# A decoder layer on one core: the roots of two layer norms on GpSimd instead of ScalarE, and the activation tables fetched elsewhere

## The reference, cut to what matters

```python
def _layernorm(x, axis=-1, eps=1e-05):
    m = jnp.mean(x, axis=axis, keepdims=True)
    v = jnp.var(x, axis=axis, keepdims=True)
    return (x - m) / jnp.sqrt(v + eps)
...
x = x + _L0_attn_ref(_layernorm(x, axis=-1), ...)
x = x + _L0_xattn_ref(_layernorm(x, axis=-1), itok_BxS_13_99985, ctx_2048, ctx_2048, ctx_2048)
x = x + _L0_ffn_ref(_layernorm(x, axis=-1), ...)
```

## Time and profile before

| | |
|---|---|
| three runs, us | 590.84, 592.22, 588.93 |
| median, us | 590.84 |
| the profiled execution, us | 591.11 |
| its span, first to last instruction, us | 589.4 |
| busy in the span | PE 511.3 (87%), PEld 453.0 (77%), DVE 426.6 (72%), ACT 288.2 (49%), POOL 233.5 (40%) |
| granted TensorE clock, mean | 0.935 |

### The profile page before, as it was taken

The page is one execution under the profiler, slowest core; times in us unless marked ns, Lnnn a source line. Parts: engine busy times, 40 slices in busy tenths (PEclk is TensorE's granted clock), DMA queues, the critical chain, the costliest instruction groups (busy, mean ns, idle before and its releaser), DMA issues.

```text
span 589.4 us, 11588 instructions
## 1 busy us (share of the span) xinstructions
PE 511.3 (87%) x3291; PEld 453.0 (77%) x3292; DVE 426.6 (72%) x967; ACT 288.2 (49%) x785; POOL 233.5 (40%) x221
## 2 busy tenths in 40 slices
PE   5899999999999999999997679997837999999800
PEld 5688898998998989989887677886625888888600
DVE  5689988989889888898899776568685444444542
ACT  2466656556666666566654625444400444444400
POOL 4307413313123042131384004445005666777773
PEclk9789999999999999999999888999875999999955
DMA  7252211202102122020072009991101455423642
GB/s 214 65 138 55 63 29 51 65 1 83 32 27 62 27 53 62 14 75 0 0 237 86 2 2 296 296 264 37 36 2 35 136 156 147 134 82 112 193 135 89
DMA packets 60893, 52.91 MB, mean 90 GB/s; under 512 B 5545, under 2 KB 58623, under 8 KB 60800
## 3 DMA queue, kind: packets, MB, share of 16 engines
q1 hardware_dynamic: 55752, 43.90, 25.3%
q0 software_dynamic: 4704, 8.44, 5.8%
q10 hardware_dynamic: 408, 0.20, 0.1%
HBM read 46.21 MB, written 14.68 MB: 103 GB/s over the span
## 4 chain that ended last, share of the span: by engine, by line
PE 54%; DVE 19%; issue 9%; POOL 9%; ACT 4%; DMA 3%; POOLq 1%; DVEq 0%; ACTq 0%
PE bank L723 14%; PE bank L724 13%; PE bank L725 13%; PE bank L893 5%; POOL yg L639 5%; POOL xg_last L628 3%; DVE qk_lo L1245 3%; PE bank L801 3%; DVE rmax L1260 3%; DVE nmax L1264 3%; PE bank L901 2%; ACT qk_hi L1082 2%; DMA x_in<-in_x 2%; ACT prob L1098 1%; DVE pT_lo L1281 1%
## 5 line engine op out<-in xcount | busy, mean ns | idle before, releaser
L527 POOL TENSOR_TENSOR w_lo<-st_c,w_hi 128x512 fp32r<-128x512 f32 x32 | 41.2, 1287 | 220.7 <-ACT w_hi L1052 220.7
L1098 ACT ACTIVATE prob<-bank,nmax 128x256 f32<-128x256 f32 x128 | 59.5, 470 | 111.2 <-DVE nmax L1264 111.2
L893 PE MATMUL bank<-moe_w,xT 128*128 x256 | 67.6, 388 | 0.0
L723 PE MATMUL bank<-hT_hi,w_lo 128*128 128x512 f32 x128 | 53.9, 421 | 7.8 <-DVE qk_lo L1245 4.2
L1340 DVE TENSOR_TENSOR hid<-bank,sg 128x128 f32<-128x128 f32 x72 | 20.9, 291 | 53.4 <-ACT sg L1164 52.7
L1245 DVE SCALAR_TENSOR_TENSOR qk_lo<-bank,b_col,qk_hi 128x512 fp32r<-128x512 f32 x64 | 47.8, 747 | 13.2 <-ACT qk_hi L1082 12.2
L1260 DVE TENSOR_REDUCE rmax<-bank 128x2 f32<-128x512 f32 x64 | 43.9, 686 | 15.8 <-PE bank L725 15.2
L1164 ACT ACTIVATE sg<-bank 128x128 f32<-128x128 f32 x72 | 19.8, 277 | 70.0 <-PE bank L893 69.9
L1273 DVE TENSOR_SCALAR prob<-prob,rinv 128x256 f32<-128x256 f32 x128 | 52.0, 448 | 2.3
L724 PE MATMUL bank<-hT_lo,w_hi 128*128 128x512 f32 x128 | 51.6, 403 | 0.0
L725 PE MATMUL bank<-hT_hi,w_hi 128*128 128x512 f32 x128 | 51.4, 402 | 0.0
(11 more groups left out here) (187 smaller groups left out, 1609.0 us busy)
## 6 DMA issues: line engine op xcount, KB each, us to landing
y_dram<-ysb SPq DMA_DIRECT2D x64, 128.0 KB, 2.4
moe_w<-in_w_gate SPq DMA_DIRECT2D x8, 512.0 KB, 8.5
moe_w<-in_w_up SPq DMA_DIRECT2D x8, 512.0 KB, 7.2
moe_w<-in_w_down SPq DMA_DIRECT2D x4, 1024.0 KB, 8.8
st_c<-in_wq_codes SPq DMA_DIRECT2D x16, 128.0 KB
st_c<-in_wv_codes SPq DMA_DIRECT2D x8, 256.0 KB
st_c<-in_wo_codes SPq DMA_DIRECT2D x8, 256.0 KB
st_s<-in_wo_scales SPq DMA_DIRECT2D x16, 128.0 KB
```

Of the source, the lines that this page charges most:

```text
L723: pe.matmul(o, l_lo, r_hi, start=start, stop=False, skip_group_check=share)
L893: mm = pe.matmul(bG[n % 2][:, 0:2 * FI], xT_of(kt), w, start=kt == 0, stop=kt == KT - 1)
L1098: ex = act.activation(prob[:, i % 4, qt, :], bS[i % 2][:, qt * S:(qt + 1) * S], ACT.Exp, bias=nmax[:, i % 2, qt:qt + 1], scale=SCALE, accu ...
```

## The change

- In the second and third norm GpSimd computes `rstd` as `var` to the power of minus one half (`ln_root`, a tensor_tensor with a constant tile of -0.5 filled at the start). ScalarE's root and VectorE's reciprocal of these two norms go. The Newton step stays. The first norm is as it was.
- The two powers of the second norm stand in GpSimd's queue ahead of the mask products, the two of the third norm behind them and ahead of the index fills.
- Behind attention's last exponential ScalarE fetches the silu table, not the square root's. Behind the shared expert's silu 1 it fetches the sigmoid's.
- The sigmoid now stands ahead of the shared expert's silu 2, and VectorE's product 2 stands behind the search for the largest scores.

```diff
@@ constants @@
+        minus_half = sb("minus_half", [P, NT])
...
-        LN_STEPS = 2 * HT + 1 + 5 + HT
+        LN_STEPS = [2 * HT + 1 + 5 + HT] + 2 * [2 * HT + 1 + 4 + HT]
+
+        def ln_done(n, half):
+
+            return 2 * sum(LN_STEPS[:n]) + (half + 1) * LN_STEPS[n]
...
@@ GpSimd @@
+        def ln_root(pool, n, half):
+
+            pool.wait_ge(v_ln, ln_done(n, half) - LN_STEPS[n] + 2 * HT + 1)
+            hs = slice(half * HT, (half + 1) * HT)
+            pool.tensor_tensor(rstd[:, hs], var[:, hs], minus_half[:, hs], ALU.pow).then_inc(p_root, 1)
...
+            pool.memset(minus_half[:, :], -0.5)
...
+            ln_root(pool, 1, 0)
+            ln_root(pool, 1, 1)
             pool.wait_ge(p_mask, 2 * NROUTE - 2)
             for n in range(RSTEPS):
...
+            ln_root(pool, 2, 0)
+            ln_root(pool, 2, 1)
             pool.wait_ge(t_y, RSTEPS)
@@ VectorE, reciprocals @@
-                dve.wait_ge(a_sd, 2 * n + half + 1)
-                k = base + 2 * HT + 1
-                dve.reciprocal(rstd[:, hs], sd[:, hs]).then_inc(v_ln, 1)
+                k = base + 2 * HT + (1 if n else 2)
+                if n == 0:
+                    dve.wait_ge(a_sd, half + 1)
+                    dve.reciprocal(rstd[:, hs], sd[:, hs]).then_inc(v_ln, 1)
+                    dve.wait_ge(v_ln, k)
+                else:
+                    dve.wait_ge(p_root, 2 * (n - 1) + half + 1)
@@ ScalarE @@
                         if pl.last and i == PAIRS - 1:
-                            fetch_table(act, ACT.Sqrt)
+                            fetch_table(act, ACT.Silu)
...
-            ln_scalar(act, 1, 0)
             ln_high(act, 1, 0, ENDS[0])
-            ln_scalar(act, 1, 1)
-            fetch_table(act, ACT.Silu)
...
-            ln_scalar(act, 2, 0)
             routed_high(RSTEPS - 1)
...
-            ln_scalar(act, 2, 1)
             silu(0, 0)
             silu(1, 1)
+            fetch_table(act, ACT.Sigmoid)
             rows_copy(1, 0)
             hidden_copy(0, 0)
             hidden_copy(1, 1)
-            silu(2, 2)
             act.wait_ge(t_r, 1)
             act.activation(score[:, :, :].rearrange("p t e -> p (t e)"), bank[0][:, 0:NT * NE], ACT.Sigmoid).then_inc(a_r, 1)
+            silu(2, 2)
             silu(3, 3)
@@ VectorE, router @@
-            product(2, 2)
...
             for t in range(NT):
                 ins = dve.max(top[:, t, :], sel[:, t, :])
             own(ins)
+            product(2, 2)
             product(3, 3)
```

More of the change, by code:

```diff
@@ L339, in decoder_layer @@
         a_sd = sem("a_sd")
+        p_root = sem("p_root")
         t_ln, a_ln, v_lnlo = sem("t_ln"), sem("a_ln"), sem("v_lnlo")
@@ L489, in _ @@
                 ts = slice(half * HT, (half + 1) * HT)
-                sp.wait_ge(v_ln, (4 + half + 1) * LN_STEPS)
+                sp.wait_ge(v_ln, ln_done(2, half))
                 sp.dma_start(h_dram.rearrange("(t p) d -> p t d", p=P)[:, ts, :], h_row[:, ts, :]).then_inc(d_h, 16)
@@ L644, in ln_vector @@
         def ln_vector(dve, n, half, src):
-            base = (2 * n + half) * LN_STEPS
+            base = ln_done(n, half) - LN_STEPS[n]
             tiles = range(half * HT, (half + 1) * HT)
@@ L662, in reciprocals @@
             def reciprocals():
-                dve.wait_ge(a_sd, 2 * n + half + 1)
-                k = base + 2 * HT + 1
-                dve.reciprocal(rstd[:, hs], sd[:, hs]).then_inc(v_ln, 1)
+                k = base + 2 * HT + (1 if n else 2)
[5 more added lines that the diff above has]
+                    dve.wait_ge(p_root, 2 * (n - 1) + half + 1)
+                dve.tensor_tensor(nt1[:, hs], rstd[:, hs], rstd[:, hs], ALU.mult).then_inc(v_ln, 1)
                 dve.wait_ge(v_ln, k + 1)
-                dve.tensor_tensor(nt1[:, hs], rstd[:, hs], rstd[:, hs], ALU.mult).then_inc(v_ln, 1)
+                dve.tensor_tensor(nt1[:, hs], nt1[:, hs], var[:, hs], ALU.mult).then_inc(v_ln, 1)
                 dve.wait_ge(v_ln, k + 2)
-                dve.tensor_tensor(nt1[:, hs], nt1[:, hs], var[:, hs], ALU.mult).then_inc(v_ln, 1)
+                dve.tensor_scalar(nt1[:, hs], nt1[:, hs], -0.5, 1.5, ALU.mult, ALU.add).then_inc(v_ln, 1)
                 dve.wait_ge(v_ln, k + 3)
-                dve.tensor_scalar(nt1[:, hs], nt1[:, hs], -0.5, 1.5, ALU.mult, ALU.add).then_inc(v_ln, 1)
+                dve.tensor_tensor(rstd[:, hs], rstd[:, hs], nt1[:, hs], ALU.mult).then_inc(v_ln, 1)
                 dve.wait_ge(v_ln, k + 4)
-                dve.tensor_tensor(rstd[:, hs], rstd[:, hs], nt1[:, hs], ALU.mult).then_inc(v_ln, 1)
-                dve.wait_ge(v_ln, k + 5)
             def rows():
@@ L687, in ln_scalar @@
         def ln_scalar(act, n, half):
-            act.wait_ge(v_ln, (2 * n + half) * LN_STEPS + 2 * HT + 1)
+            act.wait_ge(v_ln, ln_done(n, half) - LN_STEPS[n] + 2 * HT + 1)
             hs = slice(half * HT, (half + 1) * HT)
@@ L700, in ln_tensor @@
                     t = half * HT + i
-                    pe.wait_ge(v_ln, (2 * n + half + 1) * LN_STEPS - HT + i + 1)
+                    pe.wait_ge(v_ln, ln_done(n, half) - HT + i + 1)
                     mm = pe.transpose(banks[kt][:, i * P:i * P + P], h_row[:, t, kt * P:kt * P + P], ident[:, :])
```

## The result

The changed kernel takes 593.62 us, the kernel before 589.03 us (medians of 18 runs each). The ratio is put at 1.0065, 95% interval 1.0045 to 1.0085, which is 2.7 to 5.0 us slower, with 3.8 in the middle; the two medians by themselves lie 4.6 us apart. The prediction said 594.1 us, +3.27, and slower as the likeliest side. The interval leaves no doubt of slower, but its lower end is under the 0.5% that the prediction took as the least that a measurement can tell.

The account below looks back on a forecast made before the run. Mostly matmul (TensorE 54% of the chain), but VectorE's third-norm steps, the logits and GpSimd's gather set the end. 0.14 - 0.05 + 2.98 + 0.2 = +3.27 on 590.84 gives 594.1 us; 8-in-10 range 587.3 to 598.0.

Parts of the forecast that it names:

- D: Third norm, half 1: variance no longer held by index fills, but `h_row` held by them instead; +2.98 us.
- X: Time of one GpSimd power on 128x4, not in the trace: taken as 0.5 us, bounds 0.188 and 1.30.
- A: Second norm, half 0: power and two hand-overs replace root and reciprocal; +0.14 us, generally X - 0.36.
- C: Third norm, half 0: root's table load goes, but the power delays VectorE's low part; -0.05 us, generally X - 0.55.
- B: Second norm, half 1: root and a table load leave the first silu's way, covered by TensorE's matmuls; nothing.
- E: Router: sigmoid table load already hidden by the logits, product 3 starts one pitch later before the index search; +0.2 us.
- the first: Rival at third norm, half 1: fills don't hold `h_row`; time 587.2 to 588.6 us; chance 0.2.
- The second: Rival on the power: slow, computed element by element, 2 to 3 us each; time 598.6 to 601.6 us; chance 0.1.
- The third: Rival at third norm, half 1: two or three rows get through between `iota_s` and `iota_tc`; 592.0 us; chance 0.15.

Follow-up runs that it names:

- e1: Changed kernel with one more wait, so GpSimd's four index fills start only after the last `h_row` of D; ratio to the kernel before 0.9944.
- e6: Kernel before with the power in the third norm alone, second norm and router as before; ratio to before 1.0033, once more 1.0032.
- e11: Changed kernel with an unused 128x32 power on constants between D's power and the index fills; ratio to the kernel before 0.9928.
- e3: Kernel before with only the change's new router order; ratio to before 0.9924, once more 0.9995.
- e4: Changed kernel with the router's order as before and no fetch of the sigmoid table; ratio to the kernel before 1.0049.

## Why the prediction was right, point by point

The sum named the right term, and its total, +3.27, is near the measured +3.8 and the stretch's +3.47. But three of its terms were mis-sized, and they cancel, which is luck: with the power's true time alone put in, the sum would have been +4.8. That 594.1 lies so near 593.62 is luck as well. It started from the 590.84 of three runs, 1.8 above the median of 18, and added a difference 1.3 smaller than that of the medians.

- **D, right in mechanism and size.** With the measured power the prediction's own terms give -2.12 + (0.12 + 1.01 - 0.49) + 4.97 = +3.49; the profile has +3.46. It put the last row 8.2 us behind the first Newton product, and it ends 8.18 behind (407.57 to 415.75). e1, e6 and e11 show that this is the fills and that it is the third norm.
- **X, the price of a power, mis-sized.** The power was taken as 0.5 us, near the 128x4 copy's 0.188, because "the start of the instruction should be most of it". It is 1.01, inside the bounds, and e11 makes plain why the copy was the wrong neighbour: by the estimate there most of it is the elements, 4 x 0.157. A is then +0.69 and not +0.14 (1.17 against 0.48 us); its formula X - 0.36 gives +0.65.
- **C, the step that failed.** "It reads SBUF as the mask product does", so a power would hold the low part until it ends. It doesn't: `pT_lo` started at 398.71 beside the power of 398.67 and took 0.70. From the start of the variance to the Newton product it is 2.39 us instead of 2.91, so C gained 0.52, where the prediction's X - 0.55 would make it lose 0.46 at the measured X.
- **B, nothing, right in the total.** The rows there were held by mask products for 2.0 us, which the prediction didn't see; its cover, TensorE's matmuls, took it up.
- **E, right alone, short in company.** The order costs 0.20 us by itself (e3), as predicted, but 0.46 in the changed kernel, where product 3 starts 0.46 behind product 2 and not 0.2, with 0.17 of it idle and released by nothing that the profile shows. All five kernels that have powers in both norms and the new order show it (2.73 or 2.74 us from score to search). Why is open. That the sigmoid's load was hidden is right; e4 shows it.
- **TensorE, left out.** In this pair of profiles about 0.6 us came back that no term named: some 0.3 between A and D (A's +0.69 and C's -0.52 should make +0.17, and the profile has -0.11) and 0.35 between the last row and the score. Neither repeats in the other profiles (55.38 to 56.86 us for the first on unchanged code, 4.78 to 5.53 for the second with D's rows held alike, by where the clock came back). Nothing shows that these 0.6 us belong to the change, and so this part of the agreement is luck too.

Together: 3 x 0.51 for X, -0.98 for C, +0.26 for E and -0.63 for TensorE make +0.18, which with 3.27 is the stretch's 3.45 to within rounding.

Of the rivals, the first (the fills leave `h_row` alone) fell by its own mark: the first `h_row` of D took 4.02 us and not 0.4. The rule of the Trainium skill (SBUF — State Buffer, SBUF: two separate sides) beside it frees a VectorE operation with two SBUF inputs from a GpSimd operation that doesn't read SBUF. The trace agrees for the Newton product at 407.77, 0.16 us beside `iota_e`; `h_row`, one tile with two scalars per partition, was held and so isn't such an operation. The second (2 to 3 us a power) fell on its figure, though its reason, computed element by element, is what e11 points to. The third fell: the second row was held by `iota_tc` until 415.12.

## What to carry to other kernels

Work that nobody waits for isn't free where it stands: before moving a wait into a queue, list what is queued behind it and ask which operation of the other engine each of these will now meet. Here one wait ahead of the fills was worth more (0.9%) than the whole rearrangement of roots and tables cost (0.65%), in both kernels. And when a disputed operation's price is bounded by a neighbour, choose one that does the same arithmetic, or measure it at two sizes.

## What the runs showed of the hardware that was not expected

- A GpSimd power on 128x4 takes 1.01 us (1.05 at A) and on 128x32 5.41 us, and it holds neither a tensor_tensor of VectorE with two SBUF inputs (0.70 us beside it, as alone) nor a tensor_scalar (four rows in 1.38 us).
- GpSimd's multiplication of 128x512 does hold VectorE (`var` 1.04 us at 397.55, instead of 0.17; four rows 3.42 us at 356.56, instead of 1.38), though both it and the power read and write SBUF. The Trainium skill (SBUF — State Buffer, SBUF: two separate sides) has the port pair held by a GpSimd operation for its whole instruction. The traces agree for the fills and the products, and not for the power.
- A fill, which reads nothing, holds a tensor_scalar from SBUF to SBUF until it ends, in every profile here in which the two met: 4.02 us for a row of 0.41. The router's maxima (0.84 us for eight) and its index search (0.18) ran beside fills in e1 and were not held.
- One idle piece of 4.55 us was followed by 12 us of TensorE at half clock though it was busy all the time, while with 4.48 and 1.72 us of idle time and one transpose between them the clock was back at 1.00 by 419, under 4 us after the last of it.
